# Filler matmuls of constants at TensorE's waits in the first two batches of an attention layer

## The chip, the cores and the metric

The kernel runs on one core of a Trainium2 chip, as one program with one launch. The metric is device time in microseconds (us) of one execution. TensorE (PE in the rows, PEld for its weight loads) multiplies into eight banks of PSUM; VectorE (DVE), ScalarE (ACT) and GpSimd (POOL) do the elementwise work, and SyncE (SP) starts the DMAs. The engines run their own instruction streams in order and meet through semaphores.

## The reference

The input is 16 batches of 256 tokens with 128 features. Per batch it computes:

```python
g, v = x @ Wg.T + bg, x @ Wv.T + bv          # 16 heads of 8 features
corr = (g @ g.T) / (|g| |g| + 1e-8)          # per head, window of 128 back, causal
corr = (corr * mask + 1) / 2
denom = mean(corr, axis=3) + 0.5
fitness = 1 / (denom * sum(1 / denom))
attn = softmax(corr * fitness, outside the window -1e10)
x = layernorm(x + (attn @ v) @ Wo.T + bo)
h = silu(fp4(x) @ fp4(w_gate).T) * (fp4(x) @ fp4(w_up).T)
x = layernorm(x + fp4(h) @ fp4(w_down).T)
```

`fp4` quantises blocks of 16 values to a grid of eight magnitudes and back.

## The kernel before, in words

Each engine has a block of its own, and all walk the same loop over steps `t` from -3 to 20. In step `t` the batches in flight are at different stages: genes and values (the projections g and v) of batch t+3, window sums and fitness of batch t+2, scores and values of batch t, and the tail (projection, layer norm, quantised gate, up and down) of batches t-1 to t-5. The order inside a step is written out by hand, and each engine executes it in order, so a waiting instruction holds everything behind it on its engine.

On TensorE (`def _(pe)`, L738) the steps that matter here are these.

- `genes_values(t)` (L845) makes g and v of batch t+3 in bank WA. ScalarE then squares g (L683) and copies both out (L688). From the squares VectorE makes a first guess of 1/|g| (L1131 to L1137), `newton` on GpSimd refines it with twelve small operations in a row (L476 to L494), VectorE forms the unit genes `gh` (L1324), and GpSimd writes them as `A16` (L546, L557).
- `window_sums(t)` (L868) multiplies `A16` by a constant window and waits for GpSimd's second write of `A16`. VectorE turns the sums into `rden` (L1403 to L1416).
- `fitness_sums(t)` (L881) waits for `rden` and sums it over partitions. VectorE makes `rtot`, `fit` and `Bf` from it (L1285 to L1299), and `Bf` becomes `B16`, which SP transposes by DMA into `BT`; `A16` goes the same way into `AT`.
- `scores(x, p)` (L767) makes two heads of batch x in two of the three banks of S. It waits for the transposed tiles at p = 0, and otherwise for the exponentials (L596, ScalarE) that free the banks.
- `values(x, c)` (L793) multiplies four heads' exponentials by v into bank OT; `values_back` (L814) turns the result around in WA, and VectorE normalises it into `attn` (L1356, L1360).
- `genes_values` of steps t >= 0 writes WA as well, so it waits until VectorE has made `attn` of batch t-1 (L850).
- `project` (L826) makes x + attention projection in bank WB.

Scores of batch 0 begin in step -1 with heads 0 to 3, and go on in step 0; those of batch 1 are step 1. Gate, up and down work begins in step 2. VectorE prepares the weights of those in steps 0 and 1 (`weights_to_scale` behind `gh` in step 0; `weights_exponent`, `weights_round` ahead of `attn` and `weights_grid`, `weights_scaled` behind it in step 1). Bank WD holds nothing until `turn_gate_up_weights` (L748) in step 2.

The constants that the change uses are there before: `ident16`, a 128 by 128 identity in float16, and `mask16`, a 128 by 384 mask in float16, both written by GpSimd at the start; `c_pool` reaches 17 when the mask is complete.

Of the kernel before, what the change touches and what calls it, by code (L numbers as in the profile page):

```python
# [78 lines left out]
def layer(nc, x, x_turned, wgvT, WoT, bg, bv, bo, w_gate, w_up, w_down, out):  # L79
    with ExitStack() as ctx:  # L80
# [230 lines left out]
        def live(x):  # L311

            return 0 <= x < B
# [424 lines left out]
        def _(pe):  # L738
# [28 lines left out]
            def scores(x, p):  # L767

                if not live(x):
                    return  # L770
                if p == 0:
                    pe.wait_ge(s_A, 32 * (x + 1))
                    pe.wait_ge(s_B, 32 * (x + 1))
                need(pe, s_exp, H * x + 2 * p - 1)
                pair = [(2 * p + k, (H * x + 2 * p + k) % 3) for k in range(2)]
                for kt in range(NT):
                    for hd, bank in pair:
                        r, c = 32 * (head(hd) % 4), head(hd) // 4
                        for k0 in range(0, P, KG):
                            at, n = (k0, P + KG) if kt == 0 else (T + k0, P - k0)  # L780
                            q = kt * P + k0
                            pe.matmul(S[k0:k0 + KG, bank, at:at + n], AT[r:r + 32, x % 2, c, q:q + KG],  # L782
                                      BT[r:r + 32, x % 2, c, q:q + n], start=(kt == 0), stop=False)
                near = mask16[:, :].rearrange("p (b c) -> p b c", c=P)
                for n, (hd, bank) in enumerate(pair):
                    m = 32 * (head(hd) % 4)
                    for k0 in range(0, P, KG):
                        i = pe.matmul(S[k0:k0 + KG, bank, 0:SCW].rearrange("p (b c) -> p b c", c=P)[:, :, k0:k0 + KG],  # L788
                                      ident16[m:m + KG, m:m + KG], near[m:m + KG, :, m:m + KG],
                                      start=False, stop=True)  # L790
                    i.then_inc(s_sc, 1)

            def values(x, c):  # L793

                if not live(x):
                    return
                if c == 0:
                    pe.wait_ge(s_gvc, x + 1)
                    if x == 0:
                        pe.wait_ge(c_pool, 20)  # L800
                    if 2 <= x < GVR:
                        pe.wait_ge(s_pad, x - 1)
                pe.wait_ge(s_exp, H * x + 4 * c + 4)
                if c % 2 == 0:
                    need(pe, s_ot, 2 * x + c // 2)
                for kt, (q0, q1) in enumerate(((0, T), (T, SCW))):
                    for g in range(4):
                        at = VP * (2 * H * (NT * (x % GVR) + kt) + H + head(4 * c + g)) - OW * (c % 2)
                        i = pe.matmul(OT[VP * g:VP * (g + 1), T - (q1 - q0):T], gv_flat[:, at:at + VP],  # L809
                                      Pm[:, (GROUPS * x + c) % PR, g, q0:q1],  # L810
                                      start=(kt == 0 and c % 2 == 0), stop=(kt == 1 and c % 2 == 1))
                i.then_inc(s_pv, 1)

            def values_back(x):  # L814
# [8 lines left out]
                        i = pe.transpose(WA[:, o:o + P], OTs[:, half, n * P:(n + 1) * P], identf[:, :])  # L823
                i.then_inc(s_ob, 1)

            def project(t):  # L826

                after_last(pe, (t + 2, s_fit, 7 * (t + 2) + 1), (t - 2, s_y1, NT * (t - 2) + NT))
                for k in range(NT):
                    pe.matmul(WB[:, k * D:(k + 1) * D], xT[:, (t - 1) % XR, k * P:(k + 1) * P], identf[:, :],  # L830
                              start=(k == 0), stop=False)
                pe.wait_ge(s_xac, t)
                for k in range(NT):
                    pe.matmul(WB[:, k * D:(k + 1) * D], xaT[:, k * P:(k + 1) * P], woT[:, :],
                              start=False, stop=False)
                pe.matmul(WB[:, 0:T].rearrange("p (n d) -> p n d", n=NT), ones16[:, :],
                          bias16[:, D:2 * D].rearrange("p (a d) -> p a d", a=1).to_broadcast([P, NT, D]),
                          start=False, stop=True).then_inc(s_wo, 1)
# [52 lines left out]
            for t in range(FIRST, LAST + 1):  # L891
                if t > 0:
                    scores(t, 0)
                if live(t - 3):
                    if t < B:
                        pe.wait_ge(s_h, NT * (t - 3) + 1)
                    else:
                        pe.wait_ge(s_exp, H * B)
                        if t > B:
                            pe.wait_ge(s_h, NT * (t - 4) + 2)  # L900
                    gate_up(t - 3, 1, *gate_up_at(t - 3, 1))

                if t == 2:
                    turn_gate_up_weights()

                if t > 0:
                    scores(t, 1)
                values(t - 1, 3)

                scores(t, 2)  # L910
                if live(t - 4):
                    after_last(pe, (t - 3, s_h, h_done(t - 3)))
                    for k, bank in enumerate((WC, WD if t <= B else S[:, 2])):
                        pe.wait_ge(s_hq, NT * (t - 4) + k + 1)
                        for n in range(3):
                            i = pe.transpose(bank[:, n * P:(n + 1) * P], hq[:, k, n * P:(n + 1) * P], identf[:, :])
                        i.then_inc(s_hqT, 1)

                scores(t, 3)
                if live(t - 1):  # L920
                    values_back(t - 1)
                values(t, 0)

                if t == 2:
                    turn_down_weights()

                scores(t, 4)
                if live(t - 4):

                    for k in range(NT):  # L930
                        pe.wait_ge(s_hqTc, NT * (t - 4) + (k + 1 if t > B else NT))
                        for n, (k0, kn) in enumerate(KC):
                            i = pe.matmul(WD[:, k * D:(k + 1) * D], hqT[0:kn, k, n * P:(n + 1) * P], wdT[0:kn, n, :],  # L933
                                          start=(n == 0), stop=(n == 2))
                    i.then_inc(s_dn, 1)

                scores(t, 5)
                if t == -1:
                    pe.wait_ge(c_pool, 17)
                    scores(0, 0)  # L940
                wc_last = ((t - 4, s_hqTc, NT * (t - 4) + 1), (t - 3, s_h, h_done(t - 3)),
                           (t - 2, s_xac, t - 1 + (t > B)))
                if t == -1:
                    window_sums(t)
                    scores(0, 1)
                    fitness_sums(t)
                if live(t + 3):
                    genes_values(t)
                if live(t + 2) and t != -1:
                    window_sums(t)  # L950
                if live(t - 1):

                    after_last(pe, *wc_last)
                    pe.wait_ge(s_attn, t)
                    for k in range(NT):
                        i = pe.transpose(WC[:, k * P:(k + 1) * P],
                                         attn[:, k * H:(k + 1) * H, :].rearrange("p h d -> p (h d)"), identf[:, :])
                    i.then_inc(s_aT, 1)
                if t == B:
                    project(t)  # L960
                if live(t - 2):

                    after_last(pe, *wc_last)
                    pe.wait_ge(s_xq, 7 * (t - 2) + 7)
                    for k in range(NT):
                        i = pe.transpose(WC[:, T + k * P:T + (k + 1) * P], xm[:, k * D:(k + 1) * D], identf[:, :])
                    i.then_inc(s_xqT, 1)
                values(t, 1)

                scores(t, 6)  # L970
                if live(t - 2):

                    if t == 2:
                        pe.wait_ge(c_dve, 15)
                    pe.wait_ge(s_xac, copied(t) + (t == B))
                    after_last(pe, (t - 4, s_ln2, 5 * (t - 4) + 1), (t - 3, s_h, h_done(t - 3)))
                    gate_up(t - 2, 0, *gate_up_at(t - 2, 0))

                scores(t, 7)
                if live(t - 1) and t < B:  # L980
                    project(t)
                if live(t + 2) and t != -1:
                    fitness_sums(t)
                values(t, 2)
# [678 lines left out]
```

## Time and profile before

| | us |
|---|---|
| median of 3 runs | 336.33 |
| lowest and highest | 336.30 and 337.07 |
| profiled execution, its time | 335.8 |
| its span, first to last instruction | 333.8 |
| PE busy in the span | 264.9 (79%) |
| DVE busy | 253.2 (76%) |
| ACT busy | 213.0 (64%) |
| POOL busy | 198.6 (59%) |
| mean granted TensorE clock | 0.955 |

In a timeline each row is a run of equal instructions: its start, its length, the engine, the line, the tile written and read, the shapes and the count, and in brackets the engine's idle time before it and what ended it. A float32 matmul is recorded as two instructions.

### The profile page before, as it was taken

How to read it: one execution, taken by the hardware profiler on the slowest of the kernel's cores; microseconds unless marked ns; L12 is line 12 of the kernel's file. 1: busy time of each engine (PE TensorE's matmuls, PEld its weight loads, DVE VectorE, ACT ScalarE, POOL GpSimd, SP SyncE). 2: the span in 40 equal slices, each digit the busy share in tenths (PEclk: the TensorE clock that was granted, in tenths of full speed). 3: DMA queues.
4: the chain of work that ended last, by engine and by line, in shares of the span. 5: the costliest groups of instructions: out<-in, count | busy, mean ns of one | idle time of the engine just before them, and what ended most of it. 6: DMA issues, size and time to landing. Idle time of an engine off the chain costs nothing. (4 is left out here: it accounts for less than half of the span.)

```text
span 333.8 us, 12978 instructions
## 1 busy us (share of the span) xinstructions
PE 264.9 (79%) x5044; PEld 177.6 (53%) x5044; DVE 253.2 (76%) x697; ACT 213.0 (64%) x515; POOL 198.6 (59%) x471
## 2 busy tenths in 40 slices
PE   5515778989798998989898989998989999635541
PEld 3313344655466665757575666666656665514330
DVE  5723369476989898989898899999888897836631
ACT  2101535586869787877878787978788896433231
POOL 6363545346485778686869686777873553442541
PEclk9999999999999999999999999999999999975855
DMA  4032112122123313340522233223312100010000
GB/s 120 16 63 50 32 33 49 36 49 51 33 50 35 60 24 84 29 86 20 81 34 65 45 57 40 61 66 34 51 33 60 26 20 18 0 32 2 16 16 21
DMA packets 42884, 14.19 MB, mean 43 GB/s; under 512 B 35586, under 2 KB 42820, under 8 KB 42820
## 3 DMA queue, kind: packets, MB, share of 16 engines
q1 hardware_dynamic: 42820, 13.33, 20.8%
q8 instruction: 41, 0.67, 0.8%
q14 instruction: 23, 0.19, 0.2%
HBM read 2.84 MB, written 2.10 MB: 15 GB/s over the span
## 5 line engine op out<-in xcount | busy, mean ns | idle before, releaser
L596 ACT ACTIVATE Pm<-S 128x384 f32<-128x384 f32 x256 | 112.2, 495 | 51.4 <-PE S L788 51.2
L809 PE MATMUL OT<-Pm,gv 128*32 128x256 f32 (+1 forms) x1024 | 58.3, 348 | 0.0
L782 PE MATMUL S<-BT,AT 32*32 32x160 f16 (+4 forms) x2048 | 41.0, 224 | 16.9 <-ACT Pm L596 10.6
L511 POOL TENSOR_TENSOR hq<-hm,hs 128x352 f32<-128x352 f32 x32 | 24.9, 795 | 36.8 <-DVE hm L1234 36.8
L782 PEld LDWEIGHTS S<-BT,AT 32*32 32x32 f16 x2048 | 17.8, 88 | 50.6 <-ACT Pm L596 34.3
L933 PE MATMUL WD<-wdT,hqT 128*128 128x128 f32 (+1 forms) x192 | 29.0, 307 | 14.7 <-ACT hqT L664 14.7
L809 PEld LDWEIGHTS OT<-Pm,gv 128*32 128x32 f32 x1024 | 27.6, 113 | 20.9 <-issue 8.2
L933 PEld LDWEIGHTS WD<-wdT,hqT 128*128 128x128 f32 (+1 forms) x192 | 25.8, 213 | 17.4 <-ACT hqT L664 17.4
L788 PE MATMUL S<-mask,ident 32*32 32x96 f16 x1024 | 31.3, 207 | 0.0
L853 PE MATMUL WA<-wgv,xT 128*128 128x256 f32 x64 | 22.8, 489 | 4.6 <-DMA bgrow<-bg_dram 3.5
L505 POOL TENSOR_TENSOR hn<-h,hrn 128x352 f32<-128x352 f32 x32 | 25.4, 815 | 1.3
L842 PE MATMUL WC<-wguT,xaT 128*128 128x352 f32 x58 | 24.9, 511 | 0.9 <-ACT xaT L696 0.5
L520 POOL TENSOR_TENSOR rstd<-ve,mhalf 128x2 f32<-128x2 f32 x32 | 23.1, 723 | 0.0
L602 ACT ACTIVATE yo<-y,nb,rstd 128x128 f32<-128x128 f32 x32 | 14.0, 491 | 13.0 <-POOL nb L522 13.0
L843 PE MATMUL WD<-wguT,xaT 128*128 128x352 f32 x58 | 21.9, 459 | 0.0
L557 POOL TENSOR_TENSOR A<-gh,A 128x512 f16<-128x512 f32 x16 | 20.4, 1277 | 0.2
L616 ACT ACTIVATE hu<-hn,off 128x352 f32<-128x352 f32 x32 | 17.6, 615 | 3.4 <-POOL hn L505 3.4
L1215 DVE SCALAR_TENSOR_TENSOR hh<-th,WC 128x352 f32<-128x352 f32 x29 | 14.4, 496 | 5.7 <-ACT th L639 5.4
L1234 DVE SCALAR_TENSOR_TENSOR hm<-hu,hn 128x352 f32<-128x352 f32 x32 | 16.9, 527 | 1.8 <-ACT hu L616 1.8
L683 ACT ACTIVATE gsq<-WA 128x256 f32<-128x256 f32 x16 | 6.2, 386 | 18.7 <-PE WA L857 14.2
L1234 DVE SCALAR_TENSOR_TENSOR hm<-hu,hm 128x352 f32<-128x352 f32 x32 | 17.1, 533 | 0.5
L853 PEld LDWEIGHTS WA<-wgv,xT 128*128 128x128 f32 x64 | 13.3, 231 | 7.7 <-POOL ones L445 3.5
(161 smaller groups left out, 633.6 us busy)
## 6 DMA issues: line engine op xcount, KB each, us to landing
xT<-x_turned_dram SPq DMA_DIRECT2D x16, 128.0 KB, 2.3
out_dram<-yo SPq DMA_DIRECT2D x16, 128.0 KB, 2.1
AT<-A SPq DMA_TRANSPOSE x32, 2.5
BT<-B SPq DMA_TRANSPOSE x32, 2.5
wf<-w_down_dram SPq DMA_DIRECT2D x1, 176.0 KB, 2.4
wgv<-wgv_dram SPq DMA_DIRECT2D x1, 128.0 KB
wf<-w_gate_dram SPq DMA_DIRECT2D x1, 128.0 KB, 2.2
wf<-w_up_dram SPq DMA_DIRECT2D x1, 128.0 KB, 2.1
```

The source lines that it names most:

```text
L505: pool.tensor_tensor(b3(hn[:, k]), b3(h[:, k]), bc(hrn[:, k], QB), ALU.mult).then_inc(s_hn, 1)
L511: pool.tensor_tensor(b3(hq[:, k, 0:I]), b3(hm[:, k]), bc(hs[:, k], QB), ALU.mult).then_inc(s_hq, 1)
L520: pool.tensor_tensor(r[:, :], ve[:, :], mhalf[:, 0:NT], ALU.pow).then_inc(s_out, 1)
L596: act.activation(Pm[:, group % PR, hd % 4, :], S[:, (H * x + hd) % 3, 0:SCW], ACT.Exp, scale=1.0 / ZS).then_inc(s_exp, 1)
L782: pe.matmul(S[k0:k0 + KG, bank, at:at + n], AT[r:r + 32, x % 2, c, q:q + KG], BT[r:r + 32, x % 2, c, q:q + n], start=(kt == 0), stop=False)
L788: i = pe.matmul(S[k0:k0 + KG, bank, 0:SCW].rearrange("p (b c) -> p b c", c=P)[:, :, k0:k0 + KG], ident16[m:m + KG, m:m + KG], near[m:m + K ...
L809: i = pe.matmul(OT[VP * g:VP * (g + 1), T - (q1 - q0):T], gv_flat[:, at:at + VP], Pm[:, (GROUPS * x + c) % PR, g, q0:q1], start=(kt == 0 a ...
L842: pe.matmul(g, lhs, wguT[:, 0:I], start=True, stop=True).then_inc(s_gate, 1)
L843: pe.matmul(u, lhs, wguT[:, I:2 * I], start=True, stop=True).then_inc(s_gu, 1)
L853: pe.matmul(WA[:, k * 2 * D:(k + 1) * 2 * D], xT[:, (t + 3) % XR, k * P:(k + 1) * P], wgv[:, :], start=(k == 0), stop=False)
L933: i = pe.matmul(WD[:, k * D:(k + 1) * D], hqT[0:kn, k, n * P:(n + 1) * P], wdT[0:kn, n, :], start=(n == 0), stop=(n == 2))
L1234: dve.scalar_tensor_tensor(out=hm[:, k], in0=hu[:, k], scalar=ROUND, in1=hm[:, k] if step else hn[:, k], op0=ALU.max, op1=op).then_inc(s_h ...
```

## The change

A helper `keep_busy(n)` issues n matmuls of the identity by the mask into 384 columns of bank WD, each complete in itself, with no wait and no semaphore. Nothing reads the result. It is called in steps -2 to 1 at places where TensorE's next instruction waits for another engine. The wait for the mask moves from step -1 to the first call, in step -2, behind `window_sums`. Per call site: 5 in step -2; 19, 6, 5 and 5 in step -1; and 3 behind each of seven score pairs in steps 0 and 1: 82 fillers in all.

```diff
+            def keep_busy(n):
+                for _ in range(n):
+                    pe.matmul(WD[:, 0:SCW], ident16[:, :], mask16[:, :], start=True, stop=True)
...
                 if t > 0:
                     scores(t, 1)
+                if 0 <= t < 2:
+                    keep_busy(3)
                 values(t - 1, 3)
                 scores(t, 2)
+                if 0 <= t < 2:
+                    keep_busy(3)
...
                 scores(t, 5)
+                if 0 <= t < 2:
+                    keep_busy(3)
                 if t == -1:
-                    pe.wait_ge(c_pool, 17)
+                    keep_busy(19)
                     scores(0, 0)
+                    keep_busy(6)
...
                 if t == -1:
                     window_sums(t)
                     scores(0, 1)
+                    keep_busy(5)
                     fitness_sums(t)
+                    keep_busy(5)
                 if live(t + 3):
                     genes_values(t)
                 if live(t + 2) and t != -1:
                     window_sums(t)
+                if t == -2:
+                    pe.wait_ge(c_pool, 17)
+                    keep_busy(5)
...
                 scores(t, 7)
+                if 0 <= t < 2:
+                    keep_busy(3)
                 if live(t - 1) and t < B:
                     project(t)
```

The same three fillers stand behind `scores(t, 3)`, `scores(t, 4)` and `scores(t, 6)`.

On TensorE's stream the first place is step -2 and the start of step -1: the window sums of batch 0 (bank WB), the fitness sums (bank WA) and the first scores (bank S). Before:

```order
L877 MATMUL WB<-A,win 128x128 x6
L888 MATMUL WA<-rden,onesf 128x16
L889 MATMUL WA<-rden,onesf 128x16
L782 MATMUL S<-BT,AT 32x160 x8
L782 MATMUL S<-BT,AT 32x128
```

With the change, whose fillers are line 829 into WD:

```order
L882 MATMUL WB<-A,win 128x128 x6
L829 MATMUL WD<-mask,ident 128x384 x5
L893 MATMUL WA<-rden,onesf 128x16
L894 MATMUL WA<-rden,onesf 128x16
L829 MATMUL WD<-mask,ident 128x384 x19
L782 MATMUL S<-BT,AT 32x160 x8
```

Five fillers now stand ahead of the fitness sums and nineteen ahead of the first scores.

The second place, on TensorE at the end of step -1, is the second score pair of batch 0, the fitness sums of batch 1 and the genes and values of batch 2 (L853, L857; L858, L862 in the change). Before:

```order
L788 MATMUL S<-mask,ident 32x3x32 x8
L888 MATMUL WA<-rden,onesf 128x16
L889 MATMUL WA<-rden,onesf 128x16
L853 MATMUL WA<-wgv,xT 128x256 x2
L857 MATMUL WA<-bgrow,onesf 128x2x128
L782 MATMUL S<-BT,AT 32x160 x8
```

With the change:

```order
L788 MATMUL S<-mask,ident 32x3x32 x8
L829 MATMUL WD<-mask,ident 128x384 x5
L893 MATMUL WA<-rden,onesf 128x16
L894 MATMUL WA<-rden,onesf 128x16
L829 MATMUL WD<-mask,ident 128x384 x5
L858 MATMUL WA<-wgv,xT 128x256 x2
L862 MATMUL WA<-bgrow,onesf 128x2x128
L829 MATMUL WD<-mask,ident 128x384 x3
L782 MATMUL S<-BT,AT 32x160 x8
```

Each of the three pieces of work now has fillers ahead of it.

The third place, on TensorE at the end of step 1, is the last score pair of batch 1, the projection of batch 0 (bank WB) and the fitness sums of batch 3. Before:

```order
L788 MATMUL S<-mask,ident 32x3x32 x8
L830 MATMUL WB<-identf,xT 128x128 x2
L834 MATMUL WB<-woT,xaT 128x128 x2
L836 MATMUL WB<-bias,ones 128x256
L888 MATMUL WA<-rden,onesf 128x16
```

With the change:

```order
L788 MATMUL S<-mask,ident 32x3x32 x8
L829 MATMUL WD<-mask,ident 128x384 x3
L835 MATMUL WB<-identf,xT 128x128 x2
L839 MATMUL WB<-woT,xaT 128x128 x2
L841 MATMUL WB<-bias,ones 128x256
L893 MATMUL WA<-rden,onesf 128x16
```

Three fillers stand ahead of the projection.

## Rows read from the trace of the kernel before

**Rows 1.** Page, 40 slices of the span: granted TensorE clock in tenths.

```profile
PEclk9999999999999999999999999999999999975855
```

**Rows 2.** Groups by form, TensorE, 0 to 50 us: busy us, mean ns.

```profile
L877 PE MATMUL WB<-A,win 128*128 128x128 f16 x18 | 2.4, 305 | 6.2 <-POOL A L557 6.2
...
L862 PE MATMUL WA<-bias,ones 128*128 128x256 bf16 x1 | 0.4, 421 | 0.0
```

**Rows 3.** Groups by form, TensorE, 64 to 80 us.

```profile
L877 PE MATMUL WB<-A,win 128*128 128x128 f16 x6 | 0.5, 219 | 0.0
...
L862 PE MATMUL WA<-bias,ones 128*128 128x256 bf16 x1 | 0.3, 273 | 0.0
```

**Rows 4.** Timeline of TensorE, 14 to 35 us: start us, length us.

```profile
14.46 0.82 PE L877 MATMUL WB<-A,win 128*128 128x128 f16 x6 [2.29 <-POOL A L557]
17.03 0.58 PE L888 MATMUL WA<-rden,onesf 128*128 128x16 f32 x2 [1.76 <-DVE rden L1416]
17.45 0.59 PE L889 MATMUL WA<-rden,onesf 128*128 128x16 f32 x2
24.33 0.43 PE L782 MATMUL S<-BT,AT 32*32 32x160 f16 x16 [6.29 <-DMA BT<-B]
...
27.20 0.80 PE L877 MATMUL WB<-A,win 128*128 128x128 f16 x6 [2.36 <-POOL A L557]
...
29.66 0.58 PE L888 MATMUL WA<-rden,onesf 128*128 128x16 f32 x2 [1.22 <-DVE rden L1416]
...
31.01 2.08 PE L853 MATMUL WA<-wgv,xT 128*128 128x256 f32 x4 [0.35 <-DVE rtot L1285]
33.02 1.22 PE L857 MATMUL WA<-bgrow,onesf 1*128 1x256 f32 x2
```

**Rows 5.** Timeline of TensorE, 42 to 76 us.

```profile
42.78 0.80 PE L877 MATMUL WB<-A,win 128*128 128x128 f16 x6 [1.50 <-POOL A L557]
...
57.25 0.43 PE L782 MATMUL S<-BT,AT 32*32 32x160 f16 x16 [0.65 <-ACT Pm L596]
...
57.69 2.08 PE L853 MATMUL WA<-wgv,xT 128*128 128x256 f32 x4
...
61.92 0.31 PE L782 MATMUL S<-BT,AT 32*32 32x160 f16 x16
...
62.96 0.31 PE L782 MATMUL S<-BT,AT 32*32 32x160 f16 x16 [0.69 <-ACT Pm L596]
...
63.24 0.71 PE L830 MATMUL WB<-identf,xT 128*128 128x128 f32 x4
...
64.34 0.29 PE L888 MATMUL WA<-rden,onesf 128*128 128x16 f32 x2
64.49 0.37 PE L889 MATMUL WA<-rden,onesf 128*128 128x16 f32 x2
...
65.58 0.31 PE L782 MATMUL S<-BT,AT 32*32 32x160 f16 x16
...
72.38 1.13 PE L853 MATMUL WA<-wgv,xT 128*128 128x256 f32 x4
...
75.34 0.31 PE L782 MATMUL S<-BT,AT 32*32 32x160 f16 x16
```

**Rows 6.** Timeline of VectorE, 39 to 57 us.

```profile
39.74 0.42 DVE L1324 TENSOR_TENSOR gh<-gv,rn 128x256 f32<-128x256 f32 x1 [4.13 <-POOL rn L494]
...
50.08 0.80 DVE L1324 TENSOR_TENSOR gh<-gv,rn 128x256 f32<-128x256 f32 x1 [1.51 <-POOL rn L494]
...
56.32 0.42 DVE L1360 TENSOR_TENSOR attn<-WA,orec 128x256 f32<-128x256 f32 x1
```

**Rows 7.** Windows near the end: PE, PEld, DVE, ACT, POOL busy, granted clock, DMA.

```profile
303.00:307.00 4.00, 3.27 (x14) 2.95 (x14) 1.59 (x4) 2.01 (x5) 0.40 (x1) 0.50 0.00 0
310.00:314.00 4.00, 1.93 (x12) 1.27 (x12) 2.37 (x5) 1.99 (x5) 2.16 (x6) 0.99 0.11 33
314.00:316.00 2.00, 1.77 (x9) 1.47 (x7) 1.53 (x4) 0.00 (x0) 0.21 (x1) 0.50 0.00 0
```

More of the change, by code:

```diff
@@ L937, in _ @@
                 scores(t, 5)
+                if 0 <= t < 2:
+                    keep_busy(3)
                 if t == -1:
-                    pe.wait_ge(c_pool, 17)
+                    keep_busy(19)
                     scores(0, 0)
+                    keep_busy(6)
                 wc_last = ((t - 4, s_hqTc, NT * (t - 4) + 1), (t - 3, s_h, h_done(t - 3)),
@@ L970, in _ @@
                 scores(t, 6)
+                if 0 <= t < 2:
+                    keep_busy(3)
                 if live(t - 2):
@@ L979, in _ @@
                 scores(t, 7)
+                if 0 <= t < 2:
+                    keep_busy(3)
                 if live(t - 1) and t < B:
```

## The prediction

> **What bounds the kernel now.** I read the page first, then TensorE's groups in an early and in a later stretch, then the timelines of TensorE and VectorE for the first 76 us, and last the windows at the end, where the clock moves visibly.
>
> The page gives a full granted clock from the first slice on [rows 1]. The durations say otherwise, and here the durations decide. Up to 50 us one bfloat16 matmul of 256 columns takes 421 ns, and a 128-column window sum 305 ns [rows 2]; between 64 and 80 us the same forms take 273 and 219 ns [rows 3]. The genes and values of a batch, four records, take 2.08 us at 57.69 and 1.13 us at 72.38 [rows 5]. So TensorE runs at the lower level (1.2 GHz) from the start to about 61 us, with no record of it: the change is seen only in that a row at 61.92 already has the short time (0.31 us for sixteen score matmuls, 0.43 us at 57.25 [rows 5]). It came up right after TensorE had worked from 57.69 on without a wait.
>
> Who waits for whom in these 61 us? In step -1 TensorE waits for others: 2.29 us for GpSimd, 1.76 us for `rden`, 6.29 us for the transposed B, 2.36, 1.22 and 0.35 us [rows 4]. But the others wait for TensorE too, since each turn of that relay has one TensorE piece in it. In step 0 the chain is: genes of batch 2 (end 34.24), squares, first guess, Newton steps on GpSimd, `gh` at 39.74 after 4.13 us of waiting for `rn` [rows 6], `A16`, window sums at 42.78 after 1.50 us of waiting [rows 5]. `gh` also opens VectorE's weight work, behind which the next first guess stands, so `gh` of the next batch at 50.08 again waits for GpSimd (1.51 us) and `attn` of batch 0 comes at 56.32 [rows 6], behind more weight work. Genes of batch 4 need that `attn` (their bank is WA) and start at 57.69 [rows 5]. From step 2 on the steps repeat at the higher clock; I take it that a shift at the start of step 2 is kept to the end.
>
> **The change part by part.** *Price of a filler.* Six 128-column float16 matmuls take 0.82 us [rows 4], one of them 305 ns [rows 2]: (0.82 - 0.305) / 5 = 0.10 us per 128 columns, 0.31 us for 384. At the higher clock (0.5 - 0.219) / 5 = 0.056 us [rows 3], 0.17 us for 384. Each has its own weight load; in the window sums six loads of the same size hide in these spacings. 3, 5, 6 and 19 fillers cost 0.9, 1.55, 1.9 and 5.9 us at the lower clock, 0.5, 0.85, 1.0 and 3.2 us at the higher.
>
> *Step -2 and the 19.* The five fit into 1.76 us of waiting (1.55) and the nineteen into 6.29 us (5.9) [rows 4], so they cost nothing even if the clock never rises. The wait on the mask costs nothing: GpSimd writes the mask ahead of its first `A16`, for which TensorE waits at 14.46 anyway [rows 4]. Together with the fitness sums they make TensorE busy from 14.5 to about 24 us but for a few tenths. I expect the clock to rise between 20 and 24 us. What speaks for it: near the end the clock stood at 0.50 through 303 to 307 us while TensorE was busy 3.27 of 4.00 us, and by 310 to 314 us it is 0.99 [rows 7].
>
> *Step -1 at the higher clock.* The first scores wait for the DMA as before (24.33), the six fillers fit into the 2.36 us before the window sums, which wait for GpSimd (27.20). Then TensorE's pieces on the relay shorten: window sums 0.80 to 0.5 us (-0.3), fitness sums from 1.01 us (17.03 to 18.04, [rows 4]) to 0.52 us (64.34 to 64.86, [rows 5]) (-0.5). The five fillers before the fitness sums fit into 1.22 us. The five behind them do not: 0.85 us stand where TensorE waited 0.35 us [rows 4], +0.4 us. Genes and values of batch 2 took 31.01 to 34.24 = 3.23 us [rows 4]: 2.08 becomes 1.13 us [rows 5]; the one-row bias part (1.22 us) has no later row, it lies between 0.61 us (half) and 1.22 us, and I take 0.66 by the ratio 1.13 / 2.08; with the 0.07 us of overlap that is 1.7 us (-1.5). Sum: -0.3 - 0.5 + 0.4 - 1.5 = -1.9 us at 34.24.
>
> *Steps 0 and 1.* Newton, `gh` and the weight work do not depend on TensorE's clock, so `attn` comes 1.9 us earlier, at 54.4 to 54.85 us. That `attn` is the cover for the fillers before it: from the window sums of batch 2 to the genes of batch 4 TensorE took 42.78 to 57.69 = 14.9 us, waits included [rows 5]; scaled by 273 / 421 that is 9.7 us, and seven times three fillers between them add 3.5 us at most, so from 40.9 TensorE is there by 54.1 us, still ahead of `attn`. If the cover were gone, each three would cost 0.5 us. Genes of batch 4 start at 54.95 instead of 57.69 (-2.75): before, TensorE itself came last there, now VectorE does. From these genes to the scores behind `values` took 57.69 to 61.92 = 4.23 us; the same piece in step 2 takes 72.38 to 75.34 = 2.96 us [rows 5], with one more pair of transposes, so 2.65 to 2.96; I take 2.65 (-1.6). The last score pair waits for ScalarE 0.69 us before it [rows 5], which covers three fillers (0.5 us). Behind that pair three fillers stand ahead of the projection, which waited for nothing (63.24): +0.5 us. Sum at the first scores of batch 2: -2.75 - 1.6 + 0.5 = -3.85 us, 61.7 instead of 65.58 us [rows 5].
>
> *Steps 2 to 20* are unchanged and shift as one. At the end the clock falls in places already [rows 7], and where it falls may shift against the work; I put that at plus or minus 0.7 us, an estimate: the 3.27 us of busy time at 0.50 [rows 7] would take about half at the higher clock, and such a stretch may as well be gained as lost.
>
> The sum: the profiled execution 335.8 - 3.85 = 331.95 us. It stands 0.5 us below the median of the runs, so for the median 336.33 - 3.85 = **332.5 us**.
>
> One rule of the Trainium skill would make the gain smaller: "TensorE: Matmul & The Clock Gate", section "What's actually happening", says that for modelling the ramp penalty is under 1% of a typical span. By it no more than 3.3 of 333.8 us could come back, and the time would be 333.0 or more. The trace has a ramp of some 61 us, longer than that rule has in mind, and I stay with the sum.
>
> **The rivals.**
>
> *A. The clock falls back between bursts.* From 23 to 29 us TensorE has little but one score pair, one set of window sums and the fillers between waits, and in step 0 the wait before the window sums of batch 2 (1.50 us [rows 5]) grows by what the pieces ahead of it save, with no filler in it. For it: between 310 and 314 us TensorE was busy 1.93 of 4.00 us in short bursts, and the clock was at 0.50 from 314 on [rows 7]. Against it: the fillers leave fewer gaps in the same time. If it falls in the wait of step 0 and comes back within step 1, the pieces behind it lose their gain, window sums 0.3, fitness sums 0.5 and values about as much, so 333.5 to 334.5 us. If it falls before 29 us and returns by step 1, the five fillers ahead of the genes of batch 2 cost 1.55 - 0.35 = 1.2 us and the -1.9 is lost, but the end of step 1 still gains 1.6 us: `attn` +1.2, genes at 57.95 instead of 57.69, then -1.6 and +0.5: about 335.5 us. The same page of the Trainium skill, section "A second HAM failure mode: psum-queue depth-cycling", speaks for this rival: it tells of TensorE idling a little between groups of matmuls and the clock going back and forth. No row of the first 61 us here can show it, since no clock change is recorded there.
>
> *B. Slower: fillers at the lower clock.* If the clock is at 1.2 GHz for most of steps 0 and 1, each three cost 0.93 us. Before a wait of 0.65 us that is 0.3 us too much, and ahead of work that did not wait all of it. In step 1 seven times 0.93 us are 6.5 us, of which four waits take 2.6 us, and 1.2 us come from step -1: 5.1 us. TensorE was itself the last at the genes of batch 4, so most of that goes through; with the clock up at the end of step 1 some 2 us come back by the fillers' earlier rise: about 339 us. It decides where the clock is not up when step 1 begins. Against it: with these fillers TensorE has hardly a gap in step 1, and without them the clock rose at 61 us.
>
> *C. It does nothing.* The fillers do not raise the clock, or the start is not what sets the end, and the cover holds: 336.3 us. For the first half speaks only the record of a full clock from the start [rows 1]; against it the durations [rows 2, 3]. For the second half, that step 2 could still wait for something that has not moved; I find nothing such, as the transposes of batch 2 follow VectorE's work ahead of `attn`, which moves by 1.9 us too, and all else is released by TensorE.
>
> **How the numbers follow.** Forecast 0.62; A 0.22 (0.18 at 333.5 to 334.5, 0.04 at 335.5); B 0.08; C 0.08. A measurement of this kernel can tell about 0.3%, 1.0 us, from no change. Faster by more than that (under 335.3): forecast and most of A, 0.80. Same: C and the rest of A, 0.12. Slower: B, 0.08. The forecast's own range: fillers all hidden (-0.5) and the bias part at half (-0.05), with the end's 0.7, reach 331.2 us; the bias part unchanged (+0.55), 2.96 instead of 2.65 us and 0.7 at the end reach 334.0. The whole range takes in A: **331.0 to 335.7 us**.
>
> **What would show it.** Right: a 273 ns row for a 256-column bfloat16 matmul in step 0; fillers of about 0.17 us spacing before 24 us already; genes of batch 2 ending near 32.3 us; `gh` of batch 2 near 37.9 us; genes of batch 4 released by `attn` near 55 us; first scores of batch 2 near 61.7 us. Wrong: durations of 421 ns anywhere behind 24 us (A or B), waits for fillers in front of `project` or `values` that reach VectorE, or a start of step 2 earlier by 3.9 us with an end that is not.

## The result and the profile after

Over 19 executions each, the changed kernel took 333.4 us in the median (330.31 to 336.58) and the kernel before 337.85 us (335.21 to 339.43). The ratio is 0.9865, 95% interval 0.9835 to 0.9896: 4.6 us faster by it. (The ratios leave out executions over 1.5% above the fastest of their kernel, three of the nineteen here.) Two more comparisons of the same two kernels gave 0.991 (0.9866 to 0.9953) and 0.991 (0.9873 to 0.9946), about 3 us. The forecast was 332.5 us in a range of 331.0 to 335.7.

The spread of the change goes with the granted clock that each execution recorded: the four below 332 us have a mean of 0.949 to 0.958, the seven above 334 us one of 0.930 to 0.940.

The profiled execution took 334.2 us and its span is 332.3 us, so this one execution is only 1.5 us shorter in its span than the one of before. The page's row of the granted clock, in tenths for 40 slices, answers [rows 1]:

```profile
PEclk9997698999999999999999999999999999976855
```

The dips in the fourth, fifth and seventh slice are stretches at 1.2 GHz. Windows of the same trace (window, its length, busy us of PE, PEld, DVE, ACT and POOL with counts, granted clock, DMA share, GB/s) say where:

```profile
26.00:29.00 3.00, 1.69 (x35) 0.95 (x35) 1.17 (x4) 0.87 (x2) 1.05 (x1) 1.00 0.62 49
30.00:38.00 8.00, 8.00 (x68) 3.83 (x69) 2.35 (x7) 1.85 (x5) 1.86 (x7) 0.50 0.31 68
40.00:48.00 8.00, 6.70 (x147) 3.89 (x135) 6.74 (x14) 4.71 (x11) 3.73 (x9) 1.00 0.08 16
50.00:53.00 3.00, 3.00 (x44) 1.14 (x43) 2.42 (x3) 1.30 (x4) 2.58 (x5) 0.50 0.19 46
54.00:65.00 11.00, 10.81 (x228) 7.27 (x233) 8.80 (x20) 6.49 (x16) 4.10 (x13) 1.00 0.34 40
```

Up at 26 to 29 us, down at 30 to 38, up at 40 to 48, down at 50 to 53, up from 54 on. TensorE's timeline (start, length, engine, line, operation, tile, shapes, count, idle time and what ended it), to be held against [rows 4, 5]:

```profile
15.06 1.81 PE L829 MATMUL WD<-mask,ident 128*128 128x384 f16 x5
17.03 0.58 PE L893 MATMUL WA<-rden,onesf 128*128 128x16 f32 x2 [0.16 <-DVE rden L1441]
...
17.87 5.40 PE L829 MATMUL WD<-mask,ident 128*128 128x384 f16 x19
...
27.19 0.49 PE L882 MATMUL WB<-A,win 128*128 128x128 f16 x6 [1.43 <-POOL A L557]
...
27.90 0.99 PE L829 MATMUL WD<-mask,ident 128*128 128x384 f16 x5
29.35 0.58 PE L893 MATMUL WA<-rden,onesf 128*128 128x16 f32 x2 [0.47 <-DVE rden L1441]
...
30.20 1.76 PE L829 MATMUL WD<-mask,ident 128*128 128x384 f16 x5
31.75 1.91 PE L858 MATMUL WA<-wgv,xT 128*128 128x256 f32 x4
33.60 1.22 PE L862 MATMUL WA<-bgrow,onesf 1*128 1x256 f32 x2
...
43.37 0.49 PE L882 MATMUL WB<-A,win 128*128 128x128 f16 x6 [0.62 <-POOL A L557]
...
56.92 0.66 PE L829 MATMUL WD<-mask,ident 128*128 128x384 f16 x3
57.41 1.03 PE L858 MATMUL WA<-wgv,xT 128*128 128x256 f32 x4
...
61.65 0.61 PE L835 MATMUL WB<-identf,xT 128*128 128x128 f32 x4
...
63.88 0.31 PE L782 MATMUL S<-BT,AT 32*32 32x160 f16 x16
```

The nineteen fillers end at 23.27 not at 24.1 as at 0.33 us each (three and five of them at the lower clock take 1.14 and 1.81 us, 0.67 us for two), so the clock rose among them; the window sums at 27.19 take 0.49 us (0.80 before). Between 28.9 and 29.35 TensorE waits 0.47 us, and the fitness sums behind it take 0.58 us, as at the lower clock. The five fillers at 30.20 last 1.76 us, and the genes of batch 2 start at 31.75, 0.7 us later than before. VectorE (line numbers are 25 higher than in [rows 6]) follows them:

```profile
40.32 0.43 DVE L1349 TENSOR_TENSOR gh<-gv,rn 128x256 f32<-128x256 f32 x1 [4.13 <-POOL rn L494]
...
50.58 0.80 DVE L1349 TENSOR_TENSOR gh<-gv,rn 128x256 f32<-128x256 f32 x1 [1.83 <-POOL rn L494]
...
56.83 0.42 DVE L1385 TENSOR_TENSOR attn<-WA,orec 128x256 f32<-128x256 f32 x1
```

`gh` is 0.6 and `attn` 0.5 us late, not 1.9 us early. The genes of batch 4 still start 0.3 us earlier (57.41), and since they and the values behind them run at 2.4 GHz, the first scores of batch 2 stand at 63.88 instead of 65.58: 1.7 us gained, of which 1.5 us reach the end of the span.

### The profile page after: what moved, and what is told of

Same layout as the page of the kernel before. It is cut to its first block and busy times, and to the rows that moved or that the text cites. A ratio compares the mean times of both kernels' runs of the same rounds, so it can differ in the third digit from the quotient of the medians.

```text
span 332.3 us, 13142 instructions
## 1 busy us (share of the span) xinstructions
PE 275.7 (83%) x5126; PEld 181.6 (55%) x5126; DVE 252.3 (76%) x697; ACT 212.9 (64%) x515; POOL 199.4 (60%) x471
## 5 line engine op out<-in xcount | busy, mean ns | idle before, releaser
L809 PE MATMUL OT<-Pm,gv 128*32 128x256 f32 (+1 forms) x1024 | 55.8, 336 | 0.0
L782 PE MATMUL S<-BT,AT 32*32 32x160 f16 (+4 forms) x2048 | 39.7, 218 | 8.2 <-ACT Pm L596 6.8
L809 PEld LDWEIGHTS OT<-Pm,gv 128*32 128x32 f32 x1024 | 26.9, 110 | 20.2 <-issue 6.3
L788 PE MATMUL S<-mask,ident 32*32 32x96 f16 x1024 | 30.5, 202 | 0.0
L858 PE MATMUL WA<-wgv,xT 128*128 128x256 f32 x64 | 20.5, 449 | 4.6 <-DMA bgrow<-bg_dram 3.5
L829 PE MATMUL WD<-mask,ident 128*128 128x384 f16 x82 | 22.4, 414 | 0.0
L602 ACT ACTIVATE y<-WB,nb,rstd 128x128 f32<-128x128 f32 x32 | 12.9, 456 | 7.3 <-POOL nb L522 7.3
```

The lines of the kernel that those rows point to most:

```text
L602: act.activation(dst[:, k, :], yy[:, k, :], ACT.Identity, bias=nb[:, k:k + 1], scale=r[:, k:k + 1]).then_inc(s_done, 1)
L829: pe.matmul(WD[:, 0:SCW], ident16[:, :], mask16[:, :], start=True, stop=True)
```

## The experiments

Theory E, mine: the gain is TensorE's clock, up earlier through the fillers of steps -2 and -1. Rival L: the fillers of steps 0 and 1 carry it. Rival F: fillers in front of work cost what they win. Each run was timed against the kernel before on its own chip, of which there were three; the kernel before had medians of 336.24, 336.19 and 336.02 us on them. There were 12 executions of again, early_only, late_only, thin, steady_only and again_two, 6 of bridge_again and bridge_two, and 5 of bridge, no_five and bridge_steady. The last column is read from one profiled execution of each.

| run | median us, range | ratio to before (95%) | first scores of batch 2, us |
|---|---|---|---|
| before | see above | 1 | 65.58 |
| the change, profiled with its result | 333.4, 330.31 to 336.58 | 0.9865 (0.9835 to 0.9896) | 63.88 |
| again | 333.78, 331.8 to 337.56 | 0.991 (0.9866 to 0.9953) | 63.01 |
| early_only | 335.4, 333.09 to 340.84 | 0.9956 (0.9916 to 0.9997) | 63.33 |
| late_only | 334.15, 333.25 to 337.74 | 0.9936 (0.9898 to 0.9974) | 63.31 |
| thin | 336.76, 335.4 to 339.88 | 1.0023 (0.998 to 1.0067) | 66.61 |
| bridge | 332.26, 330.9 to 336.07 | 0.987 (0.9844 to 0.9896) | 60.62 |
| no_five | 332.87, 332.62 to 335.52 | 0.9909 (0.9888 to 0.993) | 63.46 |
| steady_only | 336.14, 335.21 to 339.54 | 0.9981 (0.9951 to 1.001) | 68.36 |
| bridge_steady | 332.53, 331.22 to 332.9 | 0.9887 (0.9861 to 0.9912) | 60.62 |
| again_two | 333.77, 330.63 to 335.71 | 0.991 (0.9873 to 0.9946) | 63.80 |
| bridge_again | 332.24, 330.96 to 334.6 | 0.9896 (0.9843 to 0.9949) | 60.71 |
| bridge_two | 330.91, 330.22 to 332.08 | 0.9837 (0.9794 to 0.9879) | 60.81 |

**thin.** The fillers keep their places and become 8 columns wide.

```diff
-                    pe.matmul(WD[:, 0:SCW], ident16[:, :], mask16[:, :], start=True, stop=True)
+                    pe.matmul(WD[:, 0:8], ident16[:, :], mask16[:, 0:8], start=True, stop=True)
```

> All 82 fillers in their places, but over 8 columns instead of 384, so TensorE is hardly busy by them. Both theories (the gain is the clock): within 1 us of before, clock up only at about 61 us. If instead it is faster by 2 us or more, the gain is not the clock but something about the instructions themselves (weight loads pulled ahead, the stream kept fed).

TensorE's timeline of thin:

```profile
17.85 0.65 PE L829 MATMUL WD<-mask,ident 128*128 128x8 f16 x19
...
58.05 2.05 PE L858 MATMUL WA<-wgv,xT 128*128 128x256 f32 x4
...
64.29 0.69 PE L835 MATMUL WB<-identf,xT 128*128 128x128 f32 x4
```

Nineteen fillers take 0.65 us, the genes of batch 4 still take the long time at 58.05, and nothing is gained. The same 82 instructions with hardly any columns do not help: what helps is TensorE's work, not the stream of instructions. This run has the earlier wait for the mask too, so the gain is not that either.

**early_only and late_only.** One part of the change each.

In early_only this goes at all seven places:

```diff
-                if 0 <= t < 2:
-                    keep_busy(3)
```

In late_only the calls of steps -2 and -1 go:

```diff
-                    keep_busy(19)
+                    pe.wait_ge(c_pool, 17)
                     scores(0, 0)
-                    keep_busy(6)
...
                     scores(0, 1)
-                    keep_busy(5)
                     fitness_sums(t)
-                    keep_busy(5)
...
-                if t == -2:
-                    pe.wait_ge(c_pool, 17)
-                    keep_busy(5)
```

> Only the 40 fillers of steps -2 and -1, none in steps 0 and 1. Theory E: at least 3 us faster than before, since the clock is up at 22 us and step 0 and 1 have work enough to keep it in most executions. Rival L: within 1 us of before, since the clock falls back at about 29 us and the fillers ahead of the genes of batch 2 cost up to 1 us.

> Only the 42 fillers of steps 0 and 1; the wait for the mask is back in step -1. Theory E: within 1 us of before, since step -1 runs at the lower clock and the first fillers of step 0 cost 0.9 us each three. Rival L: 2 to 4 us faster, as much as the whole change less at most 1 us.

Both parts gain something, 1.5 us (0.1 to 2.8) and 2.2 us (0.9 to 3.4) by their ratios. By these middle values Theory E missed both (at least 3 us, and within 1 us), and L had late_only right (2 to 4 us) and early_only not (within 1 us), though the interval of early_only reaches into that. The interval of late_only overlaps that of the whole change on the same chip (again), so what the early fillers add to the late ones is not shown by these times. TensorE in early_only:

```profile
30.54 1.03 PE L858 MATMUL WA<-wgv,xT 128*128 128x256 f32 x4
...
35.58 0.43 PE L782 MATMUL S<-BT,AT 32*32 32x160 f16 x16 [0.63 <-ACT Pm L596]
...
36.02 2.08 PE L858 MATMUL WA<-wgv,xT 128*128 128x256 f32 x4
...
40.72 0.80 PE L882 MATMUL WB<-A,win 128*128 128x128 f16 x6 [2.40 <-POOL A L557]
...
55.62 2.08 PE L858 MATMUL WA<-wgv,xT 128*128 128x256 f32 x4
...
61.00 0.71 PE L835 MATMUL WB<-identf,xT 128*128 128x128 f32 x4
```

and in late_only:

```profile
34.19 1.14 PE L829 MATMUL WD<-mask,ident 128*128 128x384 f16 x3
...
37.21 0.86 PE L829 MATMUL WD<-mask,ident 128*128 128x384 f16 x3
...
56.74 1.13 PE L858 MATMUL WA<-wgv,xT 128*128 128x256 f32 x4 [1.07 <-DVE attn L1379]
...
61.08 0.61 PE L835 MATMUL WB<-identf,xT 128*128 128x128 f32 x4
```

In early_only the genes of batch 2 are early (1.03 us long, 30.54), but behind waits of 1.07 and 0.63 us for ScalarE the clock is down at 35.58 and stays so through the genes of batch 4; they begin 2.1 us earlier at 55.62 all the same, since GpSimd's `A16` released the window sums of step 0 at 40.72 instead of 42.78 and TensorE's pieces behind them took their old time. In late_only that chain starts as late as before, the first fillers of step 0 are slow (1.14 us), the clock rises among the third three (0.86 us at 37.21), and the saving is made at the end of step 1. The two gains are different pieces of the path, so they should add if the clock lasts through both. The first scores of batch 2 fit that, in one profile each: 2.25 and 2.27 us early in these two, 4.96 us in bridge below, whose fillers are not quite the same.

**again and again_two.** The change unaltered.

> The change once more, unaltered, beside the kernel before on the same chip. Theory E (the early rise of TensorE's clock, by the fillers of steps -2 and -1, carries the gain): 3 to 5 us faster than before, and where the clock falls back between 28 and 50 us in a profile, that execution gains 2 us or less at the first scores of batch 2. Rival L (the fillers of steps 0 and 1 carry it): the same time, but with the gain at the first scores of batch 2 the same whatever the clock did before 35 us.

> The change unaltered, as the measure for the two below on the same chip: 3 to 4.5 us faster than before, with a spread of 4 us or more between its executions, since in each of them the clock falls at another place or not at all.

TensorE in again, whose profiled execution took 337.56 us, the longest of its twelve:

```profile
30.60 1.03 PE L858 MATMUL WA<-wgv,xT 128*128 128x256 f32 x4
...
40.81 0.49 PE L882 MATMUL WB<-A,win 128*128 128x128 f16 x6 [2.50 <-POOL A L557]
...
43.20 0.43 PE L782 MATMUL S<-BT,AT 32*32 32x160 f16 x16
...
56.55 1.03 PE L858 MATMUL WA<-wgv,xT 128*128 128x256 f32 x4
...
84.64 2.08 PE L858 MATMUL WA<-wgv,xT 128*128 128x256 f32 x4 [0.60 <-DVE attn L1385]
```

Here the clock lasts through step -1: the genes of batch 2 start at 30.60 (forecast: 30.6) and last 1.03 us. Then comes the bare wait before the window sums of step 0, 2.50 us, and at 43.20 the scores are slow again (0.43 us). The clock is up by 53 us, falls again in step 3 (the genes at 84.64 take 2.08 us) and once more at 196 us, and what was gained is lost. again_two has the falls of the first profile, at 29 and 49 us. In three profiles of the change the clock never lasted to the end of step 1. The first scores of batch 2 are 1.7 and 1.8 us early where it fell at 29 us and 2.6 us where it fell at 43 us. L had expected the same gain whatever the clock did before 35 us; E had expected 2 us or less with any fall between 28 and 50 us, so neither has it quite.

**no_five.** Without the five fillers ahead of the genes of batch 2.

```diff
                     fitness_sums(t)
-                    keep_busy(5)
```

> The change without the five fillers between the fitness sums and the genes of batch 2 in step -1. If these five delay the genes (0.4 us at the higher clock, 1.1 us at the lower, by the two profiles): the genes of batch 2 start at 30.2 to 31.1 us, and the time is 0.3 to 1 us shorter than the change's. If instead they are needed to keep the clock up: a fall behind 30 us in the profile and up to 1.5 us longer.

```profile
28.38 1.78 PE L829 MATMUL WD<-mask,ident 128*128 128x384 f16 x5
...
31.17 2.08 PE L858 MATMUL WA<-wgv,xT 128*128 128x256 f32 x4 [0.35 <-DVE rtot L1309]
...
61.23 0.61 PE L835 MATMUL WB<-identf,xT 128*128 128x128 f32 x4
```

In this execution, the longest of its five, the clock had fallen at 27 us already, before the place of the edit, so the genes at 31.17 do not answer the question for the higher clock; what the five cost there stays open. For the lower clock they do: from the fitness sums to the genes it is 1.22 us here (29.95 to 31.17) and 2.40 us with the five in the change's first profile (29.35 to 31.75), 1.2 us more. The ratio is that of the change, measured on another chip.

**steady_only.** The kernel before with fillers only from step 2 on. Its helper `keep_on(n, bank)` issues n matmuls of the identity by the float16 window constant, over 256 columns of the bank.

```diff
                 scores(t, 2)
+                if 2 <= t < 4:
+                    pe.wait_ge(s_fit, 7 * (t + 1) + 5)
+                    keep_on(5, WA)
...
                 scores(t, 4)
                 if live(t - 4):
+                    if t < B:
+                        pe.wait_ge(s_hqTc, NT * (t - 4) + 1)
+                        keep_on(4, WC)
                     for k in range(NT):
```

> The kernel before, with no filler up to step 1, but with fillers from step 2 on: five over 256 columns into bank WA behind the third score pair of steps 2 and 3, four into bank WC ahead of the down projection of steps 4 to 15, once ScalarE has copied the first half. If the executions of the kernel before near 339 us are those in which the clock falls in the steps 2 to 15: nearly all executions at 335 to 336.5 us, a gain of 0.5 to 1 us in the mean. If not: the two heights of 336 and 339 us stay.

No gain in the median is shown (the interval holds 1). Whether the two heights stay is not decided: one of twelve executions stands above 338 us, against five of fifteen of the kernel before on this chip, and the mean is 0.5 us lower, in the range named for the other answer. The one profiled execution, of 339.54 us, shows one way to the greater height. Up to 71 us this kernel is the one of before:

```profile
57.71 2.08 PE L858 MATMUL WA<-wgv,xT 128*128 128x256 f32 x4
...
68.36 0.43 PE L782 MATMUL S<-BT,AT 32*32 32x160 f16 x16
...
70.17 0.31 PE L782 MATMUL S<-BT,AT 32*32 32x160 f16 x16
```

The genes at 57.71 are where they were, but the clock did not rise behind them: the first scores of batch 2 stand at 68.36 (0.43 us) and only those at 70.17 are short. The kernel before had risen at 61 us in its profile. The late rise costs 2.8 us at the start of step 2; a recorded fall at 90 to 94 us comes on top. Not every long execution is of this kind. Of the 67 executions of the kernel before on the three chips 20 took over 338 us. In 7 of them the mean granted clock is 0.958 to 0.964, no lower than in the short ones, which fits a late rise that the record does not hold; in the other 13 it is 0.927 to 0.948, which means more recorded time at the lower clock, somewhere in the execution. A part of the change's gain in the median may be that its executions do not wait for the rise as the 7 do; no run shows how much.

**bridge, bridge_again, bridge_steady.** Fillers for the gaps in which the clock had fallen; bridge_again is bridge once more, and bridge_steady has the fillers of steady_only too. The three fillers ahead of the projection in step 1 are gone.

```diff
                 if t > 0:
                     scores(t, 0)
+                if t == 1:
+                    keep_busy(3)
...
                     scores(0, 0)
-                    keep_busy(6)
+                    keep_busy(13)
...
                     scores(0, 1)
-                    keep_busy(5)
+                    keep_busy(7)
                     fitness_sums(t)
-                    keep_busy(5)
+                    keep_busy(2)
                 if live(t + 3):
                     genes_values(t)
+                if t == 0:
+                    keep_busy(8)
...
                 scores(t, 7)
-                if 0 <= t < 2:
-                    keep_busy(3)
+                if t == 0:
+                    keep_busy(6)
```

> The change with the gaps filled in which the clock fell in the profiles so far: 13 instead of 6 fillers ahead of the window sums of step -1, 7 instead of 5 ahead of its fitness sums and 2 instead of 5 behind them, 8 new ones ahead of the window sums of step 0, 6 instead of 3 behind the last score pair of step 0, 3 new ones behind the first pair of step 1. Theory E (the gain is the clock, and what the change loses is what the clock loses by falling back): no fall between 22 and 62 us in the profile, first scores of batch 2 at 61.0 to 62.0 us, 4 to 6 us faster than before, 1 us or more better than the change. Rival F (fillers in front of work cost what they win): no better than the change's 3 to 4.5 us.

> The kernel of the run bridge once more. Theory E: up to the end of step 1 the clock stays up in every execution, so the first scores of batch 2 are again at 60.5 to 61 us; 0.5 to 1.5 us faster than the change in the median and with fewer slow executions. Rival F: the same as the change.

> The fillers of bridge and of steady_only together. Theory E: the two gains add, 5 to 7 us faster than before, 330 to 331.5 us in most executions. Rival F: no better than the better one of the two.

TensorE in bridge:

```profile
54.45 1.13 PE L858 MATMUL WA<-wgv,xT 128*128 128x256 f32 x4 [1.06 <-DVE attn L1389]
...
58.28 0.71 PE L835 MATMUL WB<-identf,xT 128*128 128x128 f32 x4
...
60.62 0.31 PE L782 MATMUL S<-BT,AT 32*32 32x160 f16 x16
...
67.06 0.31 PE L782 MATMUL S<-BT,AT 32*32 32x160 f16 x16 [0.69 <-ACT Pm L596]
...
68.10 1.40 PE L858 MATMUL WA<-wgv,xT 128*128 128x256 f32 x4 [0.69 <-DVE attn L1389]
69.29 0.42 PE L867 MATMUL WA<-bias,ones 128*128 128x256 bf16 x1
```

and in bridge_again, at the same place of step 2:

```profile
68.22 1.13 PE L858 MATMUL WA<-wgv,xT 128*128 128x256 f32 x4 [0.69 <-DVE attn L1389]
```

In all three profiles the clock is up from some 22 us to the end of step 1, and the first scores of batch 2 are 4.9 to 5.0 us early. In bridge it falls at 69 us, in step 2, behind bare waits of 0.69 us, and in bridge_steady too, in spite of its five fillers behind the third pair. In bridge_again it does not fall there, behind the same waits, and lasts to 290 us; its span is 329.3 us, that of bridge 330.3. Against the change on one chip (bridge_again and again_two) the median is 1.5 us shorter, but the intervals of the two ratios overlap. The fillers of steady_only add nothing that shows: bridge_steady has 0.9887, 3.8 us, against 0.987 of bridge alone, as Rival F had it; Theory E had 5 to 7 us.

**bridge_two.** The fillers of bridge, and four each at three places of step 2.

```diff
-            def keep_busy(n):
+            def keep_busy(n, bank=WD):
...
                 scores(t, 2)
+                if t == 2:
+                    pe.wait_ge(s_fit, 7 * (t + 1) + 5)
+                    keep_busy(4, WA)
...
                 scores(t, 4)
+                if t == 2:
+                    keep_busy(4, WC)
...
                 scores(t, 5)
+                if t == 2:
+                    keep_busy(4, WC)
```

> The fillers of bridge, and in step 2 four each behind the third score pair (into WA), the fifth and the sixth (into WC, free there). In two profiles with the fillers of bridge the clock fell at 69 us, behind two bare waits of 0.69 us in step 2, and TensorE's pieces up to 72 us took twice their time. If that costs the end what it costs there, this is 1 to 1.5 us faster than bridge, 5 us faster than before, with no fall before 75 us. If it is made good later by waits that shrink, or the clock then falls in step 3: the same as bridge.

```profile
54.64 1.13 PE L858 MATMUL WA<-wgv,xT 128*128 128x256 f32 x4 [1.26 <-DVE attn L1396]
...
58.48 0.71 PE L835 MATMUL WB<-identf,xT 128*128 128x128 f32 x4
...
60.81 0.31 PE L782 MATMUL S<-BT,AT 32*32 32x160 f16 x16
...
67.54 0.82 PE L829 MATMUL WC<-mask,ident 128*128 128x384 f16 x4
68.30 1.13 PE L858 MATMUL WA<-wgv,xT 128*128 128x256 f32 x4
```

The clock lasts to 286 us. Ratio 0.9837, interval 0.9794 to 0.9879: 5.5 us faster than before, median 330.91 us against 333.77 us of the change on the same chip, all six executions between 330.22 and 332.08 us. It has the lowest median of these kernels, and only two of the change's twelve executions on that chip (330.63 and 331.48) were below its slowest. What the fillers of step 2 add to those of bridge is not shown: the interval overlaps that of bridge_again (0.9843 to 0.9949), and the profile of bridge_again, without them, has the same span of 329.3 us. Three of the six executions of bridge_again are as short (330.96 to 331.2 us), the others took 333.27 to 334.6 us.

## Why the prediction was right, and where not

The time and the sign came out: 332.5 was forecast, 333.4 measured, within the range. That it came so near is in part luck, as the path to it was another than forecast. Step by step:

- *Prices.* Three fillers at the higher clock last 0.66 us with their passage and thirteen 2.29 us (bridge), 0.163 us each; the forecast had 0.17. At the lower clock 1.14 and 1.81 us for three and five, 0.33 each by the difference, against 0.31. The one-row bias part at the higher clock lasts 0.69 us (early_only), forecast 0.66. In the sum of step -1 the five fillers at 0.85 us against a wait of 0.35 us make +0.5 and not +0.4 us, which makes it -1.8 and not -1.9 us.
- *Steps -2 and -1.* Five fillers end before `rden` (17.03 as before) and nineteen before the DMA: free, as forecast. The clock rises between 20 and 24 us, as forecast. Where it lasts through step -1 the genes of batch 2 start at 30.5 to 30.6 us (again, early_only) and in again `gh` of batch 2 comes at 37.76 us; forecast 37.9.
- *The step that failed* is that the clock, once up, stays up. I gave this 0.62 and rival A, falling back between bursts, 0.22. In all three profiles of the change it fell back, at 29 and 49 us twice, once at 43 us. The falls at 29 and 43 us lie in the gaps that rival A named; that at 49 us lies behind a bare wait of 0.69 us for ScalarE at the start of step 1, which A did not name. By the prediction's own signs this is the wrong case: times of the lower clock behind 24 us. The profiled execution is near A's second case: genes of batch 2 late, `attn` late, the end of step 1 still early. I had 335.5 us for it and it took 334.2 us, since less was lost ahead of the genes of batch 4: those of batch 2 were 0.7 and not 1.2 us late. The cover failed too: the prediction had TensorE at the genes of batch 4 before `attn`, but here `attn` is done at 57.25, and the genes of batch 4 start at 57.41, right behind the three fillers ahead of them. In again, A's first case, `attn` is done at 54.92 and TensorE comes to the genes only at 56.55; A had 333.5 to 334.5 us for it, and with the falls in step 3 and at 196 us it took 337.56 us.
- *The size where the clock lasts* is right, as bridge and bridge_two show: `attn` releases the genes of batch 4 at 54.45 and 54.64 (forecast 54.95), and the first scores of batch 2 stand 5.0 and 4.8 us early. The forecast had 3.85 with 0.5 us of cost for the three fillers ahead of the projection, which these two kernels don't have, so 4.35 to compare; in bridge_two 4.5 us of it reach the end of the span (329.3 against 333.8 us). In bridge, with its fall at 69 us, 3.5 of 5.0 us do: that a shift at the start of step 2 is kept to the end holds only where the clock does not fall again behind it.
- *Why 333.4 was near 332.5 nonetheless.* From profile to profile 335.8 became 334.2 us, where the sum had 331.95 us: with the falls 2.25 us of the forecast 3.85 us were missing. The gain of 4.6 us by the first ratio is more than forecast, but there the kernel before had a median of 337.85 us, 1.5 us above the 336.33 us that I started from; the two repeats, with medians of 336.24 and 336.02 us, give 3 us. So a change that gained less than forecast in its profiles met a kernel before that was slower than in mine. Which of the nineteen executions lost the clock where cannot be seen.
- *Rivals.* B, slower by fillers at the lower clock: three of them did last 1.14 us each time in the low stretches, but those ended within 11 us (29.3 to 39.8 us in the first profile). C is refuted by the three ratios, whose intervals all end below 1, and thin shows that it isn't the instructions as such.

By the Trainium skill's rule that the ramp penalty is under 1% of a typical span ("TensorE: Matmul & The Clock Gate", section "What's actually happening") no more than 1% could be gained. bridge_two gained 1.6% (0.9837, interval 0.9794 to 0.9879), and the measurement decides. For the change itself the first ratio, 0.9865, is beyond it and the two repeats, 0.991, are not. The section "A second HAM failure mode: psum-queue depth-cycling" of the Trainium skill's same page tells, of another kernel, that TensorE idles a little between groups of matmuls and the clock goes back and forth. The trace agrees in that: down at 30 to 38, up at 40 to 48, down at 50 to 53 us.

## What to carry to other kernels

Read a fixed matmul's duration early and late in a trace before believing the clock's row: 421 ns against 273 ns was the whole finding. Filler work into a free bank can buy the higher clock, but only while the clock stays up: here it fell in the waits that the fillers had left open, not in every execution, and a part of the cover brought a part of the gain and a wide spread (330.31 to 336.58 us). And what the higher clock is worth is read from the pieces of TensorE that lie on the relay between the engines, not from its busy time.

## What the runs showed of the hardware

The record gives a granted clock of 1.00 from the start while durations are those of 1.2 GHz: the 256-column bfloat16 matmul takes 421 ns there [rows 2], and 0.42 us again at 69.29 in bridge, where the record has 0.50, against 273 ns later [rows 3]. In each of these profiles the first change that is recorded is a fall; no first rise is.

The clock fell with TensorE far from idle: in the change at about 29 us after 26 to 29 us with 1.69 of 3.00 us busy, and in again at 83 us, in step 3, behind waits of 0.69 us. The same instructions and waits do not always meet the same clock: it rose at 61 us in one execution and at 69 us in another (before, steady_only), and behind the two waits of 0.69 us in step 2 it fell in bridge and not in bridge_again.
